# New costs and priorities for the list-filling of two phases in a one-core graph-and-experts kernel

## The reference

```python
x = x + L0_gnn(norm(x), adj);  x = x + L0_ffn(norm(x))   # 6 experts, top 2
x = x + L1_gnn(norm(x), adj);  x = x + L1_ffn(norm(x))   # 4 experts, gates from a GAT over 524288 edges
x = x + L2_gnn(norm(x), adj);  x = x + L2_ffn(norm(x))   # a shared and 8 routed experts, top 2, GELU
x = x + L3_gnn(norm(x), mask, adj);  x = x + L3_ffn(norm(x))   # 8 routed experts, top 2, ReLU
```

## Time and profile before

| what | value |
|---|---|
| median of 3 runs | 2752.92 us (2751.19 to 2754.5) |
| the profiled execution | 2749.05 us |
| its span, first to last instruction | 2747.2 us |
| mean granted clock of TensorE | 0.897 of full speed |
| busy: TensorE, VectorE, ScalarE, GpSimd | 2235.4, 1780.1, 1369.2, 1295.5 us |
| instructions | 40763 |

### The profile page before, as it was taken

How to read it: one execution, slowest core, us unless ns; L and a number is a source line. 1 busy time by engine, 2 the same in 40 slices (tenths; PEclk the granted TensorE clock), 3 DMA queues, 4 the chain that set the end, 5 groups by cost and what they waited for, 6 DMA issues and landing times.

```text
span 2747.2 us, 40763 instructions
## 1 busy us (share of the span) xinstructions
PE 2235.4 (81%) x12080; PEld 1668.3 (61%) x12080; DVE 1780.1 (65%) x4750; ACT 1369.2 (50%) x3028; POOL 1295.5 (47%) x1203
## 2 busy tenths in 40 slices
PE   4979898999999898789704356989899999999980
PEld 2545555554555554456503246989888889898880
DVE  5999898787887666643467765764455666736122
ACT  3545546574756463665403244645555545354540
POOL 1010100000010475777757775427457667567776
PEclk9989999999999899999856578999999899999995
DMA  4010104000010214232232222445455465465762
GB/s 156 1 40 1 33 0 110 16 17 17 17 33 1 50 32 118 77 79 80 69 112 67 81 43 80 125 110 154 115 140 148 120 176 141 111 170 144 185 152 75
DMA packets 235139, 233.08 MB, mean 85 GB/s; under 512 B 60365, under 2 KB 185023, under 8 KB 234002
## 3 DMA queue, kind: packets, MB, share of 16 engines
q1 hardware_dynamic: 200626, 184.23, 22.9%
q0 software_dynamic: 34272, 46.02, 8.7%
HBM read 168.02 MB, written 68.45 MB: 86 GB/s over the span
## 4 chain that ended last, share of the span: by engine, by line
PE 21%; POOL 10%; issue 8%; DVE 6%; ACT 2%; DMA 2%; POOLq 1%; SPq 0%; DVEq 0%; ACTq 0%
PE bank L2241 19%; POOL got_room L83 4%; POOL room L2210 3%; POOL c_slots L2195 2%; POOL got_room L2210 1%; PE bank L440 1%; PE bank L2366 1%; DVE c_lane_hot L2635 1%; DMA got_room<-table_dram,own_rows 1%; DMA made<-c_made 1%; ACT weights_f L2460 1%; ACT L2460 0%; DVE c_token_hot L2638 0%; DMA c_slots<-sent,c_tokens_of_slots 0%; DVE c_tile_hot L2637 0%
## 5 line engine op out<-in xcount | busy, mean ns | idle before, releaser
L1011 POOL TENSOR_TENSOR a_rstd<-a_var,minus_half 128x4 f32<-128x4 f32 x64 | 93.7, 1464 | 833.3 <-DVE a_var L1565 826.3
L2195 POOL DMA_INDIRECT c_slots<-sent,c_tokens_of_slots x340 | 358.7, 1055 | 269.9 <-PE bank L2366 144.3
L1670 DVE TENSOR_TENSOR room<-room 128x768 f32<-128x768 f32 (+2 forms) x312 | 369.9, 1208 | 22.7 <-ACT room L1407 15.2
L2241 PE MATMUL bank<-c_slots_t,c_expert 128*128 128x256 f32 x1360 | 343.6, 398 | 30.0 <-ACT weights_f L2460 21.7
L2460 ACT ACTIVATE weights_f<-bank,c_expert 128x256 f32<-128x256 f32 x680 | 276.6, 469 | 178.5 <-PE bank L2241 178.4
L2241 PE MATMUL bank<-c_experts_w,weights_f 128*128 x2720 | 346.1, 283 | 4.0 <-ACT weights_f L2460 4.0
L2241 PEld LDWEIGHTS bank<-c_experts_w,weights_f 128*128 128x128 f32 x2720 | 337.8, 199 | 14.8 <-issue 10.3
L2241 PEld LDWEIGHTS bank<-c_slots_t,c_expert 128*128 128x128 f32 x1360 | 258.6, 200 | 68.8 <-issue 36.4
L1041 PE MATMUL bank<-a_h1p,weights_a 128*128 128x512 f32 x544 | 242.5, 595 | 0.0
L2657 DVE TENSOR_TENSOR c_made<-bank,c_expert 128x256 f32<-128x256 f32 x170 | 72.1, 424 | 263.0 <-PE bank L2241 249.4
L83 POOL DMA_INDIRECT got_room<-table_dram,own_rows x175 | 185.5, 1060 | 62.0 <-issue 62.0
(11 more groups left out here) (539 smaller groups left out, 4581.7 us busy)
## 6 DMA issues: line engine op xcount, KB each, us to landing
c_expert<-packed_dram SPq DMA_DIRECT2D x170, 322.0 KB, 3.4
made<-c_made SPq DMA_DIRECT2D x170, 128.0 KB
results_dram<-a_results SPq DMA_DIRECT2D x64, 256.0 KB
room<-results_dram SPq DMA_DIRECT2D x16, 1024.0 KB, 5.7
room<-in_adj SPq DMA_DIRECT2D x32, 256.0 KB, 5.1
sent<-c_rows_to_send SPq DMA_DIRECT2D x32, 256.0 KB, 2.7
c_slots<-sent,c_tokens_of_slots POOLq DMA_INDIRECT x340
a_adj<-in_adj SPq DMA_DIRECT2D x16, 256.0 KB, 3.0
```

What stands on the lines that cost most here:

```text
L1011: rstd.did(g_.tensor_tensor(st.rstd[:, :], st.var[:, :], env.minus_half[:, 0:GT], ALU.pow), what, k)
L1670: v.tensor_tensor((dv[:, :, 0, :], other(dv))[j], sv[:, :, 0, :], other(sv), (ALU.min, ALU.max)[j]).then_inc(sort_step, 1)
L2195: pool.indirect_dma_start(out=XS[p.r % S_BUFS][:, j, :], out_offset=None, in_=env.sent_dram[p.q], in_offset=bass.IndirectOffsetOnAxis(ap=T ...
L2241: return nc.tensor.matmul(out, lhsT=lhsT, rhs=rhs, start=start, stop=stop, skip_group_check=True)
```

## The change

Only constants of the filling change, no instruction. Longer figures are put in for the two VectorE steps and the TensorE step of "route", for the landing of "rows", "load2", "pull", "gather", "gather_last" and "store" in phase C, and for HOP, which holds for both phases. All offsets of PREFER_A (76 kinds of work) and PREFER_C (47 kinds) are replaced, and one entry of SHARED_AFTER is. The functions are the same.

```diff
-HOP = 0.15
+HOP = 0.25
 WHOLE = ("begin", "gates")
 PREFER_A = {
-    "adjT": (1409.0, 1591.0), "att": (3059.0, 4002.0), "begin": (-2544.0, -2748.0), "c1": (652.0, 314.0), "c2": (-1945.0, -950.0),
...
+    "adjT": (2694.0, 2366.0), "att": (4826.0, 4757.0), "begin": (-2508.0, -3003.0), "c1": (109.0, 623.0), "c2": (-1794.0, -913.0),
...
-    "route": [(DVE, 4.5), (ACTE, 0.3), (PE, 0.5), (DVE, 6.0)], "mark": [(DVE, 3.0), (PE, 0.9)], "list": [(DVE, 0.3)], "save": [(SP, 0.5)], "pull": [(POOL, 2.6)], "gather": [(POOL, 5.2)], "gather_last": [(POOL, 5.2)],
+    "route": [(DVE, 6.2), (ACTE, 0.3), (PE, 0.6), (DVE, 7.3)], "mark": [(DVE, 3.0), (PE, 0.9)], "list": [(DVE, 0.3)], "save": [(SP, 0.5)], "pull": [(POOL, 2.6)], "gather": [(POOL, 5.2)], "gather_last": [(POOL, 5.2)],
...
-LANDS = {"rows": 2.5, "load2": 6.0, "load3": 6.0, "save": 3.0, "pull": 2.5, "gather": 2.5, "gather_last": 2.5, "fetch": 5.0, "experts": 15.0, "store": 3.0}
+LANDS = {"rows": 4.0, "load2": 9.0, "load3": 6.0, "save": 3.0, "pull": 4.0, "gather": 4.0, "gather_last": 4.0, "fetch": 5.0, "experts": 15.0, "store": 5.0}
 PIECES = 4
 NORMS = ("lift", "settle", "ease", "blend")
 WHOLE_C = ("edge", "late", "route")
 PREFER_C = {
...
-    "edge": (5292.0, 1846.0), "enter_end": (-1822.0, 680.0), "experts": (-1946.0, -1935.0), "f2_score": (349.0, 825.0), "f2_xt": (-71.0, 618.0),
...
+    "edge": (5622.0, 2342.0), "enter_end": (441.0, 1547.0), "experts": (-1334.0, -4067.0), "f2_score": (982.0, 961.0), "f2_xt": (-86.0, 1050.0),
...
-SHARED_AFTER = (0, 3, 6, 15, 17, 31, 40, 96)
+SHARED_AFTER = (0, 4, 6, 15, 17, 31, 40, 96)
```

More of the change, by code:

```diff
@@ new lines @@
+    "adjT": (2694.0, 2366.0), "att": (4826.0, 4757.0), "begin": (-2508.0, -3003.0), "c1": (109.0, 623.0), "c2": (-1794.0, -913.0),
+    "clear": (-3446.0, -163.0), "comb": (57.0, -817.0), "count": (87.0, 1419.0), "cv": (894.0, -331.0), "dist": (669.0, 614.0),
+    "edge": (6484.0, -2232.0), "encode": (1008.0, 2735.0), "ends": (-2922.0, 421.0), "fall": (-597.0, 978.0), "fetch": (2409.0, 3460.0),
+    "fill": (3637.0, 3011.0), "first": (-1244.0, -2463.0), "fold": (-1080.0, -1125.0), "gate1": (-75.0, 224.0), "gate2": (698.0, 3125.0),
@@ new lines @@
+    "gate3": (5009.0, 2101.0), "gates": (1779.0, 539.0), "gb": (-1310.0, 377.0), "ghn": (4468.0, -1707.0), "gin": (1516.0, 3154.0),
+    "gt": (-139.0, 265.0), "hh": (1629.0, 992.0), "index": (933.0, -2991.0), "keep": (-19.0, -743.0), "keys": (3929.0, -723.0),
+    "l0agg": (1640.0, -1837.0), "l0out": (1415.0, -115.0), "last": (-4401.0, -1473.0), "lg": (-6145.0, 1688.0), "lists": (2570.0, 233.0),
+    "load": (-39.0, 2077.0), "loada": (435.0, -1838.0), "most": (1848.0, 1092.0), "msg": (-579.0, 623.0), "nmp": (-1309.0, -1781.0),
@@ L559 @@
+    "nn": (-1063.0, -1458.0), "norm0": (4034.0, -59.0), "norm1": (1817.0, -1010.0), "norm2": (3204.0, -1666.0), "norm3": (1271.0, 1554.0),
+    "o": (763.0, 1213.0), "ot": (2133.0, -1629.0), "out": (2617.0, 885.0), "own": (-4281.0, -2943.0), "prepare": (1015.0, 1453.0),
+    "r": (8507.0, 2989.0), "res": (-3572.0, 2613.0), "rh": (2090.0, 1819.0), "rows": (-2360.0, -1003.0), "save": (-368.0, 2279.0),
[4 rows of a table added]
 LANDS_A = {"load": 3.0, "loada": 3.0, "out": 3.0, "keys": 25.0, "save": 20.0, "first": 2.5, "lists": 6.0, "keep": 3.0, "fetch": 3.0, "last": 2.5, "rows": 2.5, "xin": 6.0, "res": 3.0, "own": 2.5}
@@ L1904 @@
 PREFER_C = {
-    "adj": (-120.0, 917.0), "agg": (682.0, -388.0), "back": (991.0, 1292.0), "blend": (3125.0, 2862.0), "blend_end": (4416.0, -1613.0),
-    "climb": (593.0, -918.0), "compare": (3056.0, 658.0), "conv": (-822.0, -527.0), "ease": (891.0, 143.0), "ease_end": (-1505.0, 5667.0),
-    "edge": (5292.0, 1846.0), "enter_end": (-1822.0, 680.0), "experts": (-1946.0, -1935.0), "f2_score": (349.0, 825.0), "f2_xt": (-71.0, 618.0),
-    "f3_score": (-6.0, 2091.0), "f3_xt": (1299.0, -488.0), "fetch": (3299.0, 1882.0), "flip": (828.0, 1167.0), "g3_xt": (1958.0, 3718.0),
@@ L1909 @@
[L1909 to L1912, removed]
@@ L1913 @@
-    "settle": (418.0, -1587.0), "settle_end": (2953.0, 3036.0), "soften": (1801.0, 5140.0), "store": (-4329.0, 2418.0), "sum": (-7342.0, 263.0),
-    "take": (6856.0, 2045.0), "xt": (-2663.0, 1751.0)}
-SHARED_AFTER = (0, 3, 6, 15, 17, 31, 40, 96)
+    "adj": (-244.0, 1373.0), "agg": (-15.0, -24.0), "back": (2555.0, 2400.0), "blend": (3154.0, 3665.0), "blend_end": (4777.0, -1079.0),
+    "climb": (924.0, -1111.0), "compare": (3372.0, 1269.0), "conv": (-1934.0, -749.0), "ease": (1172.0, 485.0), "ease_end": (-1231.0, 6765.0),
@@ new lines @@
+    "edge": (5622.0, 2342.0), "enter_end": (441.0, 1547.0), "experts": (-1334.0, -4067.0), "f2_score": (982.0, 961.0), "f2_xt": (-86.0, 1050.0),
+    "f3_score": (139.0, 2098.0), "f3_xt": (1998.0, -1588.0), "fetch": (4674.0, 2014.0), "flip": (761.0, 1118.0), "g3_xt": (1853.0, 3255.0),
+    "gather": (-3125.0, 1589.0), "gather_last": (-7376.0, -4411.0), "late": (-7556.0, 2037.0), "leave": (2168.0, 600.0), "lift": (602.0, 793.0),
+    "lift_end": (-457.0, -3998.0), "list": (3424.0, 1701.0), "load2": (5038.0, -5349.0), "load3": (-6733.0, -3892.0), "lower": (-33.0, -45.0),
@@ new lines @@
+    "mark": (2786.0, 5344.0), "mask": (-198.0, 2545.0), "mix": (3150.0, -2412.0), "project": (-52.0, -23.0), "pt": (635.0, 492.0),
+    "pull": (-178.0, -482.0), "raise": (1266.0, 1628.0), "route": (3091.0, 6913.0), "rows": (-937.0, 744.0), "save": (1232.0, 2472.0),
+    "settle": (1008.0, -1695.0), "settle_end": (3447.0, 2600.0), "soften": (-309.0, 5338.0), "store": (-4752.0, 2593.0), "sum": (-7631.0, 782.0),
+    "take": (7333.0, 1589.0), "xt": (-1025.0, 1760.0)}
+SHARED_AFTER = (0, 4, 6, 15, 17, 31, 40, 96)
```

## The result

The changed kernel takes 2776.82 us (2770.5 to 2780.4, 4 runs) beside 2752.66 for the kernel before on the same chip: a ratio of 1.0085, 95% interval [1.0065, 1.0105]. The forecast was a gain of 16 with a range of 2710 to 2768; the time lies above it.

A forecast was written before the change was run, and what follows sets the result against it. Bounds: TensorE with VectorE to 1095 us, GpSimd's gathers to 1384, no full engine in the ramp, TensorE from 1700, GpSimd for the last 94.2. Gains 9 + 3 + 4 = 16 gave 2737 us; range 2721 to 2747, 8-in-10 range 2710 to 2768.

The forecast's parts named there:

- After 1095 VectorE's 86.9 us of waiting for exponentials ... are covered by GpSimd's gathers: 0.: Phase A after 1095 us: the new hop changes nothing, since GpSimd's gathers cover VectorE's waits for exponentials and landings; 0.
- Priorities: 0, bounded by what a list has been seen to do when it is wrong, 16.5 us.: Both phases: new offsets and shared passes are a reshuffle of the same order; 0, bounds 16.5 us to either side.
- one pair of kinds in nine changes places: Phase A: comparing the offsets' middles, about this share of pairs swaps order; one in fourteen in phase C.
- The hop in phase A: 4 gained, bounds 10.: Phase A up to 1095 us: 4% of TensorE's 133.4 us standing is 5, 4 taken as gained; bounds 10 either side.
- Ramp, 9 gained.: Phase C's start, 1384 to 1700 us: longer row landings shorten ScalarE's felt hold before edge exponentials; 9 gained, bounds 0 and 36.3.
- The 66.4: Ramp of phase C: ScalarE's least hold for 16 edge pairs, 4.15 us each, of the 102.7 us it stood.
- the sign that I named: Ramp of phase C: ScalarE's wait before edge exponentials was to drop from 102.7 towards 75 us.
- Stores, 3 gained.: Layer 3's gathers on GpSimd: a pull written in front fills part of a 4.6 us store wait; 3 gained, bounds 0 and 4.6.
- Routing 0: Phase C's six routings: TensorE's 26.4 us of standing stay between 20 and 32; 0, bounds 26.4 gained and 10 lost.
- Landings 0: Phase C's gathers, pulls and load2: longer landing figures cost nothing, VectorE covers the gathers; 0, without cover 11 us lost.
- Later edge pairs in the ramp: Rival, phase C's ramp: VectorE puts another item before each edge pair, delaying the late gates; 14 us slower, 2767; chance 0.18.
- More table loads: Rival, ScalarE: the new order adds unpriced function-table reloads, ten on the path costing 13 us, 2766; chance 0.07.

The follow-up runs named there:

- b_falls_to_r: Kernel before, with four edge exponentials on ScalarE moved directly in front of a result's copy: 2749.2 us, 0.9990.
- b_most_late: Kernel before, with GpSimd's second reduction of the row counts put behind the last four gathers of own rows: 2756.4 us, 1.0021.
- tail_all: Changed kernel, with phase A's second part back in the old order on TensorE, ScalarE, VectorE and GpSimd: 2756.0 us, 1.0016.
- falls_back: Changed kernel, with only ScalarE's 19 waits and their exponentials in phase A's second part put back in their old places: 2770.8 us, 1.0063.
- c_only: Kernel before, with the new costs, hop, priorities and shared passes in phase C only: 2750.5 us, 0.9998.
- c_costs: Kernel before, with only the new durations and hop in phase C, old priorities and shared passes: 2770.7 us, 1.0077.
- a_only: Kernel before, with the new hop and priorities in phase A only: 2782.4 us, 1.0103.
- most_back: Changed kernel, with GpSimd's second reduction moved ahead of four gathers and four other gathers behind the edges' gathers: 2768.5 us, 1.0066.
- b_pool_early: Kernel before, with the last group's reciprocal root and then the second reduction moved ahead of GpSimd's last eight own-row gathers: 2753.4 us, 1.0001.
- b_both: Kernel before, with the GpSimd moves of b_pool_early and the four exponential moves of b_falls_to_r: 2747.2 us, 0.9994.
- b_most_early: Kernel before, with GpSimd's second reduction alone moved ahead of the last own-row gathers and the reciprocal root before it: 2764.7 us, 1.0046.

## Why the prediction was wrong, point by point

**"After 1095 VectorE's 86.9 us of waiting for exponentials ... are covered by GpSimd's gathers: 0."** This step failed, and with it the forecast. The cover was real but thin, and I gave it no size. Before the change VectorE waited for landings at ten pairs of 16, and in b_falls_to_r earlier exponentials turned into waits for landings; so the gathers bounded what could be gained. They don't bound what can be lost: in the changed kernel the wait for exponentials grew by 39.6 us, the wait for landings had only 35.2 to give and gave 34.2 of it, the last edge exponential came 18.3 later and the phase ended 25 later. The chain edge, exponential, edge sum runs in lockstep with L1's experts on ScalarE, and past the gathers an exponential that comes later is felt to the end: the term should have been the lateness that the new lists give these exponentials, less that slack. A reduction that is late ahead of the gathers is not covered by them either (b_most_late, 5.1 us). Phase A ended at 1409.7, not between 1374 and 1384.

**"Priorities: 0, bounded by what a list has been seen to do when it is wrong, 16.5 us."** The bound was mis-sized. A single wait bounds one wrong place; new offsets move many, and alone they cost 43 us in phase A and 22 in phase C. The reading of the offsets' middles ("one pair of kinds in nine changes places") also failed as a measure: a few places in four lists decide (tail_all), and ScalarE's 19 alone don't (falls_back).

**"The hop in phase A: 4 gained, bounds 10."** Alone it costs 42; with the new offsets it gains 13 over them. It can't be priced without them.

**Ramp, 9 gained.** (The 66.4 is reckoned with the new hop; with the old one it is 64.8, and the term stays at 9.) The late gates start 6.1 earlier, so the start moved about as forecast. But the sign that I named was wrong: ScalarE's wait rose from 102.7 to 149.7, and those waits cost the gates nothing. What failed is that an earlier ramp makes the phase shorter: the first routing came 14.5 later, and TensorE's full stretch did not begin earlier (114.8 us of work in the ramp, 136.1 before). c_only puts the whole of phase C at 0 within 0.1%.

**Stores, 3 gained.** The stall went as forecast (0.9, under 2), the time did not: the last run of gathers starts 1265.7 us after the first edge gather before and 1266.6 after. In the changed kernel no store holds its start: it stands 0.30 us behind GpSimd's last pull, and the pulls and gathers ahead of it follow each other 1.31 us apart.

**Routing 0:** right, 26.4 and 25.7. **Landings 0:** nothing speaks against it, but it was tried only with the other durations of phase C (c_costs). **The rivals.** Later edge pairs in the ramp: no, earlier. More table loads: no, the four groups have 60 now, 62 before:

```profile
L1360 ACT ACT_TABLE_LOAD x21 | 26.9, 1283 | 0.4
L1478 ACT ACT_TABLE_LOAD x16 | 20.5, 1283 | 0.3
L2460 ACT ACT_TABLE_LOAD x15 | 19.2, 1283 | 8.0 <-PE bank L2241 7.8
...
L2436 ACT ACT_TABLE_LOAD x8 | 10.3, 1283 | 0.1
```

That rival looked at the right thing from the wrong side: the price lies in where the switches stand, not in how many there are. Whether "the table of costs has no entry for it" is the cause is not shown, as no list here was filled with such an entry, and the kernel before has the same table. The cost table gives an edge exponential 0.45 us of ScalarE where the trace shows 2.9 (two loads of 1.28 and 0.36), and the reduction 2.0 where it shows 6 to 12.

What stays open: the 5 us in front of the second part, what fills the time in front of the reduction, which of the new durations delays the first routing, and why the new lists of phase C show no gain beside the old phase A (c_only) and 5.6 beside the new one (2782.4 for a_only, 2776.8 for the changed kernel; their intervals overlap).

## What to carry to other kernels

Before a wait is called covered, ask how much later it can get before it is felt: see what the waiting engine stood for at each step, and how often that was the covering one (here ten pairs of 16 before, one after). Cover bounds the gain of an earlier piece; it gives a later one only its slack. Where lists are filled from durations and tuned offsets, the two belong together; new durations with offsets made for the old ones cost 0.8 to 1.5% here. A cost that the table lacks or has too low (a table switch, a reduction) is worth putting in, with offsets made for it; no run here tried that. When a piece is moved forward on an in-order engine, name what it now stands in front of: moving the reduction alone cost 14 us because a reciprocal root was queued behind it.

## What the runs showed of the hardware

GpSimd's reduction over the partitions, the second of the two "most", has a record of 0.45 us, with 6.09 to 12.17 us in front of it in which nothing is shown, whether a root or a gather came before. Behind a root it is 7.78 (the kernel before), 6.43 (tail_all), 6.55 (most_back), 12.17 (b_pool_early) and 11.39 (b_both); behind gathers 10.50 (the changed kernel), 9.11 (b_most_early) and 6.09 (b_most_late). The root that came after one reduction and four gathers had 7.08 us in front of it (b_most_early). The Trainium skill, GPSIMD Engine Reference, Instruction dispatch, says that the first call of freshly loaded GpSimd code costs about 6 us with no instruction in the profile. The smallest gaps agree with that; no run here shows code being loaded, and it does not explain 12.17.

TensorE's granted clock fell behind a stand as short as 3.56 us: 16 products took 3.43 us instead of 2.05 (the rows of piece two).
